# Cross-attention on one core: every engine's program stands in a new, finer order

## The reference

```
Q = x @ Wq + bq ; K = ctx @ Wk + bk ; V = ctx @ Wv + bv        (512 x 1024 each)
scores = (Q_h @ K_h^T) / 8 * mask                              per head, 512 x 512
attn = softmax(scores) ; ctx_h = attn @ V_h
x = x + concat(ctx_h) @ Wo + bo
out = (x - mean) / sqrt(var + 1e-5) * gamma + beta
```

## Time and profile before

| | |
|---|---|
| median of 3 runs | 3216.45 us (3216.22 to 3218.16) |
| profiled execution, own time | 3215.79 us |
| its span | 3213.9 us |
| granted TensorE clock, mean | 0.909 |
| busy PE / DVE / ACT / POOL | 84% / 67% / 56% / 36% |

### The profile page before, as it was taken

One profiled execution on the slowest core, in us unless ns is written; L12 is line 12 of the kernel. 1 busy time (PEld: TensorE's weight loads), 2 busy tenths in 40 slices (PEclk: granted clock), 3 DMA queues, 4 the chain that ended last, 5 costly groups with the idle time before them and its releaser, 6 DMA issues.

```text
span 3213.9 us, 49972 instructions
## 1 busy us (share of the span) xinstructions
PE 2698.6 (84%) x14336; PEld 1834.1 (57%) x14336; DVE 2139.6 (67%) x4128; ACT 1807.4 (56%) x3809; POOL 1157.6 (36%) x1671
## 2 busy tenths in 40 slices
PE   6888888988888988888888878888788888888876
PEld 4555655555555655655555555555556555555554
DVE  5666666666666666666666766676666776667764
ACT  4655555555555555555565555555555555555553
POOL 2333333333333333333233434344333443434433
PEclk8989999999999999999999899898998988999888
DMA  5666556666556666656766565565655656556563
GB/s 154 131 149 152 123 125 145 155 146 154 126 122 152 148 150 151 129 120 154 183 160 126 129 139 136 124 150 125 141 134 133 148 130 140 134 127 148 128 138 92
DMA packets 1165324, 446.04 MB, mean 139 GB/s; under 512 B 1078880, under 2 KB 1078880, under 8 KB 1165280
## 3 DMA queue, kind: packets, MB, share of 16 engines
q1 hardware_dynamic: 1162160, 445.49, 62.1%
q10 hardware_dynamic: 3120, 0.01, 0.1%
HBM read 143.41 MB, written 33.55 MB: 55 GB/s over the span
## 4 chain that ended last, share of the span: by engine, by line
DVE 27%; PE 25%; ACT 19%; issue 16%; SPq 6%; DMA 4%; POOL 2%; DVEq 1%; ACTq 1%; POOLq 0%
DVE p L620 14%; ACT probs L463 11%; DVE score_ps L606 6%; PE fill_ps L297 5%; PE fill_ps L298 5%; PE fill_ps L299 5%; PE ctx_ps L365 4%; SPq L228 4%; DMA raw<-in_ct 4%; ACT p L475 4%; PE score_ps L343 2%; ACT q_hi L454 2%; PE score_ps L349 2%; PE score_ps L346 2%; DVE v_rest L643 1%
## 5 line engine op out<-in xcount | busy, mean ns | idle before, releaser
L463 ACT ACTIVATE probs<-score_ps,neg_max 128x512 f32<-128x512 f32 x1024 | 690.7, 685 | 886.9 <-POOL neg_max L804 886.9
L620 DVE SCALAR_TENSOR_TENSOR p<-probs,inv_sum,p 128x512 f16<-128x512 f32 x1024 | 946.1, 977 | 204.1 <-ACT p L475 204.1
L475 ACT ACTIVATE p<-probs,inv_sum 128x512 f16<-128x512 f32 x1024 | 655.9, 711 | 220.5 <-DVE inv_sum L614 220.5
L365 PE MATMUL ctx_ps<-pT,v 128*64 128x512 f16 x5120 | 611.9, 397 | 99.3 <-DVE ctx_lo L627 90.5
L606 DVE CUSTOM_DVE_ANT_0 score_ps<-score_ps,mask_sb 128x512 f32<-128x512 f32 x1024 | 676.7, 715 | 21.9 <-PE score_ps L349 20.9
L804 POOL TENSOR_SCALAR neg_max<-row_max 128x2 f32<-128x2 f32 x512 | 116.4, 227 | 1253.1 <-DVE row_max L606 1252.1
L365 PEld LDWEIGHTS ctx_ps<-pT,v 128*64 128x64 bf16 x5120 | 293.3, 114 | 403.7 <-issue 96.4
L343 PE MATMUL score_ps<-k_hi,q_hi 64*128 64x512 f32 x1024 | 305.6, 498 | 223.1 <-DVE k_lo L636 138.0
L297 PE MATMUL fill_ps<-xT_hi,wq_hi 128*128 128x512 f32 x512 | 245.1, 479 | 165.0 <-DVE v_rest L643 147.9
L343 PEld LDWEIGHTS score_ps<-k_hi,q_hi 64*128 64x128 f32 x1024 | 130.9, 204 | 366.7 <-issue 235.5
L636 DVE SCALAR_TENSOR_TENSOR q_lo<-fill_ps,bq_col,q_hi 128x512 fp32r<-128x512 f32 x128 | 95.9, 750 | 260.5 <-ACT q_hi L454 260.5
(11 more groups left out here) (60 smaller groups left out, 4551.5 us busy)
## 6 DMA issues: line engine op xcount, KB each, us to landing
raw<-in_xt SPq DMA_DIRECT2D x128, 256.0 KB, 3.3
raw<-in_ct SPq DMA_DIRECT2D x128, 256.0 KB, 3.6
mask_sb<-in_mask_Bx1xSxS_fk SPq DMA_DIRECT2D x128, 256.0 KB, 3.2
acc<-in_x SPq DMA_DIRECT2D x64, 256.0 KB, 3.4
partial<-acc SPq DMA_DIRECT2D x64, 256.0 KB, 2.6
acc<-partial SPq DMA_DIRECT2D x64, 256.0 KB, 3.3
out<-acc SPq DMA_DIRECT2D x64, 256.0 KB, 2.4
pT<-p SPq DMA_TRANSPOSE x512, 4.5
```

Source lines behind the costliest of these rows:

```text
L365: mm = nc.tensor.matmul(ctx_ps[a * DH:(a + 1) * DH, :], v_piece[piece][:, t, col:col + DH], pT[:, par, :, a, plane, t, :], start=is_first, ...
L463: nc.scalar.activation(probs[:, i % 4, :], score_ps[:, i % 4, :], ACT.Exp, bias=neg_max[:, p % 2, i:i + 1], accum_out=row_sum[:, p % 2, i: ...
L475: nc.scalar.activation(p16[:, q, a, 0, :], probs[:, i % 4, :], ACT.Copy, scale=inv_sum[:, p % 2, i:i + 1]).then_inc(p_rounded, 1)
L620: nc.vector.scalar_tensor_tensor(out=p16[:, q, a, 1, :], in0=probs[:, i % 4, :], scalar=inv_sum[:, p % 2, i:i + 1], in1=p16[:, q, a, 0, :] ...
```

## The change

No operation is added or taken away, and the buffers are the same: `E_TILES` is 4, as before, and `POOL_TILES` is empty, so that the new `split_probs` on POOL is never called. Three things differ.

- Every engine's `body(prev, here, nxt, ...)` is a new list. It runs once more than before: round `here` is done together with what is left of `prev` (O2, O3, the norm) and with pairs 0, 1 and most of pair 2 of `nxt`. The prologue is the same list with `nxt` alone, the end the same list with `prev` alone.
- Helpers take ranges of single tiles, and the list interleaves them: masks of coming tiles stand between splits of the present ones, scores stand one query tile at a time between fills.
- `FILL_BANK` follows the new order of fills. Semaphores are parted to allow it (`xc_split` in two, new waits of `evacuate` on the scores and values that still read its target), and V0 may stand ahead of other fills.

The core of the diff: the new list of PE, a stretch of those of DVE and of POOL, and the start of SP's.

```diff
-FILL_BANK = dict(zip("O0 O1 K3 O2 O3 Q0 Q1 K0 K1 Q2 K2 V0 V1 V2 V3 Q3".split(),
+FILL_BANK = dict(zip("O2 O3 Q0 Q1 K0 K1 V0 V1 Q2 K2 Q3 V2 V3 O0 K3 O1".split(),
                      (0, 1, 2, 0, 1, 2, 0, 1, 2, 0, 1, 2, 0, 1, 2, 1)))
...
+            def body(prev, here, nxt, out_weights, weights):
...
+                if prev:
+                    fill(prev, "O", 2)
+                if here:
+                    scores(here, 2, range(3, 4))
+                    values(here, 0)
+                    scores(here, 3, range(0, 2))
+                if prev:
+                    fill(prev, "O", 3)
+                if nxt:
+                    fill(nxt, "Q", 0)
+                    fill(nxt, "Q", 1)
+                if here:
+                    scores(here, 3, range(2, 4))
+                    values(here, 1)
+                if nxt:
+                    fill(nxt, "K", 0)
+                    fill(nxt, "K", 1)
+                    scores(nxt, 0, range(0, 2))
+                if here:
+                    values(here, 2)
+                if nxt:
+                    scores(nxt, 0, range(2, 3))
+                    fill(nxt, "V", 0)
+                    scores(nxt, 0, range(3, 4))
+                    fill(nxt, "V", 1)
+                    scores(nxt, 1, range(0, 1))
+                if here:
+                    values(here, 3)
+                if nxt:
+                    scores(nxt, 1, range(1, 2))
+                    fill(nxt, "Q", 2)
+                    fill(nxt, "K", 2)
+                    scores(nxt, 1, range(2, 3))
+                    fill(nxt, "Q", 3)
+                    scores(nxt, 1, range(3, 4))
+                    fill(nxt, "V", 2)
+                    fill(nxt, "V", 3)
+                    scores(nxt, 2, range(0, 2))
+                if here:
+                    fill(here, "O", 0)
+                if nxt:
+                    fill(nxt, "K", 3)
+                    scores(nxt, 2, range(2, 3))
+                if here:
+                    fill(here, "O", 1)
...
+                if here:
+                    scale_sums(here, 2, 0)
+                    split_value(here, range(3, 4))
+                    negate_max(here, 2, range(2, 3))
+                if nxt:
+                    split_input(nxt, "x", range(1, 2))
+                if here:
+                    negate_max(here, 2, range(3, 4))
...
+                if weights is not None:
+                    load_weight(weights, "q")
+                if weights is not None:
+                    load_weight(weights, "k")
+                if weights is not None:
+                    load_weight(weights, "v")
+                if nxt:
+                    load_input(nxt, "x", range(0, 1))
```

More of the change, by code:

```diff
@@ L22 @@
 XC = 2 * DT
+E_TILES = 4
+POOL_TILES = ()
+VECTOR_TILES = tuple(i for i in range(TILES) if i not in POOL_TILES)
 SCORE_SCALE = 1.0 / 8.0
@@ L150, in out_no, with split_done @@
             return n * QT + q + 1
[L152 to L155, removed]
+        def split_done(n, p, i):
+            eng, tiles = ("gpsimd", POOL_TILES) if i in POOL_TILES else ("vector", VECTOR_TILES)
+            return p_split[eng], (n * PAIRS + p) * len(tiles) + tiles.index(i) + 1
         def fill_read(n, kind, k):
@@ L185, in _, with load_input @@
         def _(sp):
[L186 to L189, removed]
+            def load_input(at, t, tiles):
+                g, b, n = at
+                for i in tiles:
+                    if i == 0 and not (isinstance(n, int) and n == 0):
+                        if t == "x":
+                            wait_alone(sp, qk_ready["Q"], pair_no(n - 1, PAIRS - 1))
+                        else:
+                            wait_alone(sp, qk_ready["K"], pair_no(n - 1, PAIRS - 1))
+                            wait_alone(sp, v_ready, n * KT)
                     sp.dma_start(raw_input(t, i), (xt if t == "x" else ct)[b, i * P:(i + 1) * P, :]).then_inc(
@@ L233, in prologue @@
[L233 to L285, removed]
@@ L432, in _ @@
             batches(pe, body)
-            for q in range(QT):
-                fill(LAST, "O", q)
         @block.scalar
@@ L589, in _ @@
+            for n, vec in (("q", bq), ("k", bk), ("v", bv)):
+                with nc.allow_non_contiguous_dma(reason="once, 1024 values to columns"):
+                    act.dma_start(bias_col[n][:, :], vec.rearrange("(j p) -> p j", p=P)).then_inc(bias_in, DMA)
+            for dst, vec in ((bo_b, bo), (gamma_b, gamma), (beta_b, beta)):
+                act.dma_start(dst[:, :], vec.partition_broadcast(P)).then_inc(rows_in, DMA)
             batches(act, body)
-            for q in range(QT):
-                standardize(LAST, q)
@@ new lines, in scale_and_shift @@
+            def scale_and_shift(at, tiles):
+                g, b, n = at
+                if g == 1:
+                    for q in tiles:
+                        i = (n - B) * QT + q + 1
+                        pool.wait_ge(centered, i)
+                        nc.gpsimd.tensor_tensor(acc[:, q, :], acc[:, q, :], gamma_b[:, :], ALU.mult).then_inc(scaled, 1)
+                        pool.wait_ge(scaled, i)
+                        nc.gpsimd.tensor_tensor(acc[:, q, :], acc[:, q, :], beta_b[:, :], ALU.add).then_inc(normed, 1)
```

933 lines of the change are left out of this document (507 added, 426 removed).

## The result

The change takes **2552.68 us** (median of 4, 2551.73 to 2553.46) against 3216.34 us before; the ratio is 0.7937, 95% interval 0.7923 to 0.7950, 664 us or 20.6% less. I had forecast 2687 us with a range from 2560 to 2860.

What follows compares the result with a forecast made beforehand. It took a ring of waits to bound the kernel, then PE: 88 + 15 x 80 + 86 + 15 x 83 + 66 = 2685 us of span, 2687 us predicted, range 2560 to 2860.

Steps and rivals of the forecast that it cites:

- What bounds the kernel: A ring of waits across engines holds a round at 96.4 us in group 0; the change passes the bound to PE.
- The ring: Masks, exponentials, roundings and splits waiting on each other between DVE and ACT: eight steps a round, 12.0 us each.
- PE's own time: PE's fills, scores and values at full clock: 44.8 + 12.6 + 17.8 = 75.2 us a round.
- How much is left: Waits left on PE in a round: 5 us in group 0, 8 in group 1, giving 80 and 83 us.
- the crowded half: PE's list from V1 to pair 2's last scores, 36 us; DVE 90% full there, 97% in group 1.
- The ends: Outside the regular rounds: values of round 0 at 88 us, step between the groups 86, tail 66.
- the rule: VectorE with two SBUF inputs and GpSimd share an exclusively locked port pair; closer packing makes more DVE splits slow.
- rival 1: DVE becomes the bound through slow splits, mean well over 977 ns: 2846 us at half the added length; chance 0.14.
- The signs I had named: Rounds of 80 and 83 us, PE over 90%, clock near 1.0, exponentials' wait below 10 us, DVE near 80%.
- The worst wait of PE one on DVE: A sign that the forecast is right: PE's longest wait would be for DVE.
- PE's floor: The lower end of the range, 2560 us, taken as the run time that PE's work allows.
- rival 2: Nearly PE's own time, only one late place left: rounds of 76.5 and 78.5 us, 2559 us; chance 0.18.

Runs made afterwards that it cites:

- b_less_pe: The kernel before with one of the three products of every fill left out on PE; 3106.66 us, ratio 0.9650.
- b_masks: The kernel before with only DVE's masks of tiles 4 to 7 moved ahead of the splits of tiles 0 to 3 in each pair; 2940.41 us, ratio 0.9139.
- a_less_pe: The changed kernel with one of the three products of every fill left out on PE; 2314.28 us, ratio 0.7187 to the kernel before.
- a_dve8: The changed kernel with 8 more DVE operations a round in four places of the crowded half; 2558.53 us, ratio 0.7945 to the kernel before.

## Why the prediction was wrong

**What bounds the kernel: right.** The ring of masks, exponentials and splits held a round at 96 us; b_less_pe shows that PE's work hardly counted (3.5 of 14.6 us), b_masks that the masks behind the splits did (8.1 us of a round). That the bound would pass to PE is what the profile after and a_less_pe show.

**PE's own time: 75.2, measured 76.87.** The term was 2% short. I took scores at half of a block of two and a fill at the mean of two in a row. The new list has single query tiles between fills. In its timeline, before the fill V0 and before the next score:

```profile
960.96 0.50 PE L384 MATMUL score_ps<-k_hi,q_hi 64*128 64x512 f32 x2
...
961.85 0.50 PE L336 MATMUL fill_ps<-wv_hi,cT_hi 128*128 128x512 f32 x1
...
964.80 0.50 PE L384 MATMUL score_ps<-k_hi,q_hi 64*128 64x512 f32 x2
```

A query tile and a fill take 964.80 - 960.96 = 3.84 us, not 0.79 + 2.80 = 3.59. Over the round from 1005.6 to 1082.5 us the starts in the timeline add up to 17.75 us of values, 13.5 of scores (0.80 us where two query tiles follow each other, 0.89 where one stands alone, eight of each) and 45.6 of fills (2.72 to 2.95 each). I had 17.8, 12.6 and 44.8; the 0.9 and 0.8 us are the 1.7.

**How much is left: the step that failed.** I added 5 us in group 0 and 8 in group 1 to PE's time; the runs show 1.7 in both, and those are PE's own time from the paragraph above, not waits: in the windows after PE is busy in all of a round, and its matmuls wait for nobody in four rounds. The reason I gave was DVE at 90 and 97% of the crowded half. The windows after show that half:

```profile
928.80:965.70 36.90, 36.90 (x243) 23.92 (x241) 29.40 (x61) 25.47 (x55) 15.88 (x21) 1.00 0.87 191
965.70:1005.60 39.90, 39.90 (x210) 28.19 (x208) 32.29 (x65) 29.01 (x63) 20.38 (x27) 1.00 0.73 162
```

DVE's 32.3 us were right (I had 32.6), but the stretch from V1 to the last scores of pair 2 is 39.9 us, not 36: 81%. Most of that was a miscount: the ten fills, eight query tiles and one pair's values in it make 38.8 us at my own prices. And the deeper error: I turned a busy share into waits. a_dve8 put DVE to 91% of that half, the share that I had feared, and the round moved 0.3 us. (80 - 75.2) x 15 and (83 - 75.2) x 15 are 189 us of the sum, against 30 x 1.7 = 50 measured: 139 us too much, more than the 133 us of span by which the forecast missed.

**The ends.** Start 81.4 (I said 88), step between the groups 84.9 (86), tail 70.5 (66). The sum of these is 3 us under mine, by luck: the start came 6.6 us earlier than I said and the tail 4.5 us later. I had not seen that neighbouring rounds pay too, 83.3 and 77.7 at the step and 78.7 for the first one: 9 us. With the 139 us above, 139 + 3 - 9 = 133 us, the whole miss.

**Slow splits: the rule held, the rival did not.** The mean split fell from 977 to 885 ns where rival 1 wanted it to rise, and DVE was not the bound. I had looked for the price of the lock on DVE alone; POOL's negations paid it, 227 to 458 ns in the mean, where it hid.

**The signs I had named:** the clock near 1.0, PE over 90%, exponentials waiting under 10 us a round and DVE near 80% all came. "The worst wait of PE one on DVE" did not: the only one left is on ACT's exponentials, and hidden.

**The range** ended at 2560, and I called that PE's floor. It was not: 75.2 us in each of the 30 rounds with the ends of rival 2 make 2489 us. It was rival 2's own time, 2559, so that about half of a case with a chance of 0.18 lay outside. A case that counts needs its own spread inside the range.

## What to carry to other kernels

When each engine runs a fixed list, first compute the fullest engine's own time from its list, the time at changes from one kind of matmul to another included, and then ask of each late result by how many microseconds it may be late: a busy share of 81 to 91% on a neighbour meant 0 to 0.3 us of waits on the bound here. Test slack with dummy work, at the place in question: 5 us on DVE were free here and 11 were not. Moving masks ahead of splits paid by itself (8.6%), while two further edits in the same spirit made it worse; parts of a schedule do not add up, and each has to be measured with what it is to stand beside.

## What the runs showed that I had not expected

- Packing the same work into 21% less time made the slow splits on DVE fewer (over 1300 ns 206 before, 122 after, mean 977 to 885 ns) and POOL's negations twice as long (227 to 458 ns). With 8 us more of small POOL operations the slow splits were fewer still (100, mean 859).
- Giving PE less work in the kernel before lowered its granted clock, from 0.93 to 0.85 in a round; of 467 us of matmul time left out, PE's busy time fell by 351, and the run by 115.
- Scores one fill earlier on PE cost 90 us. The weight loads of the scores then wait for exponentials, 17.4 us in 300 where it was 2.6, with the fill behind them; the later context inputs may share in it.
